# Mixture of experts: dense over all tokens, against rows sorted by expert through DRAM

## The chip, the cores and the metric

One core of a Trainium2 chip runs the whole program once. The metric is the device time of one execution in microseconds, the median of three runs. Engines are PE (matrix products), DVE (vector), ACT (scalar), POOL (general purpose) and SP, which here only issues DMAs.

## The reference, cut to what matters

Two transformer layers work on 32 x 141 = 4512 tokens of width 128. The change is in the last block, a mixture of 8 experts of hidden width 256 with the best 2 chosen for each token, and a shared expert that all tokens pass:

```python
xt = x.reshape(Bb * Ss, D)
shared = jax.nn.silu(xt @ sw1) * (xt @ sw3) @ sw2
scores = xt @ gate_w.T
_, idx = jax.lax.top_k(scores + biases, K)          # K = 2 of E = 8
topv, _ = jax.lax.top_k(scores, K)
p = jax.nn.sigmoid(topv)
p = p / jnp.sum(p, axis=-1, keepdims=True)
h = jax.nn.silu(jnp.einsum('td,edh->eth', xt, w1)) * jnp.einsum('td,edh->eth', xt, w3)
y = jnp.einsum('eth,ehd->etd', h, w2)
comb = jnp.einsum('tk,tke->te', p, onehot)
out = jnp.einsum('te,etd->td', comb, y) + shared     # + h outside
```

The reference itself computes every expert for every token and weights six of eight with zero.

## The kernel before, in words

The engines run programs of their own and meet by semaphores; the order on each engine is the order in which its lines are written. The residual stream `hT` and the normed input `xn` lie in SBUF with the feature on the partition and all 4512 tokens along the row. Until the last layer norm ("lnm") the kernel computes the tokens, the first attention, a merged feed-forward and the second attention; the change leaves those stages as they are, apart from a barrier point (`cleared`) at which semaphores of early stages are set to zero and used again, and from the layout of the expert weights `wparts`.

All fp32 products of the last block are made of three products in the type fp32r: a value is split into a high part (a cast) and a low part (value minus high part), and high x high, high x low and low x high are added up in PSUM (`three`, lines 876 to 879).

**Router.** In "lnm", chunk by chunk (12 chunks of 376 tokens), PE multiplies the gate weights by the chunk (L417), ACT copies the 8 x 376 scores (L425), PE turns them in four pieces (L413), and DVE gathers them (L431). POOL makes the low part of the input (L601). Then DVE computes the choice and the shares in one chain of dependent ops over 94 x 384 values (L1339 to L1395), PE turns the matrix of shares (L858), and ACT and DVE copy it.

**Expert stage.** For each chunk there are 18 units: 2 halves of the hidden width for each of the shared expert and the 8 experts. In one unit PE makes 3 gate-up products and 3 up products (L877 to L879); ACT applies silu (L1075); DVE multiplies by the share of the expert, which PE has broadcast to all partitions (L910, L1420), and by the up product (L1424); ACT casts the high part (L1068); POOL subtracts for the low part (L609); and PE makes 3 down products three units later, summed over all 18 units in one PSUM bank. Behind each chunk DVE adds the residual (L1407), PE turns the result in four pieces (L873), ACT copies it (L1063) and SP stores it (L401). The store's SBUF side is 94 partitions of 4 x 128 values, its DRAM side rows of 128 values:

```python
o = out.rearrange("b n d -> (b n) d").rearrange("(c s p) d -> c p s d", s=NSUB, p=SUB)   # SUB = 94, NSUB = 4
...
sp.dma_start(o[bass.ds(c, 1)].rearrange("a p s d -> (a p) s d"), m_o[0:SUB]).then_inc(S("stored"), 16)
```

Of the kernel before, what the change touches and what calls it, by code (L numbers as in the profile page):

```python
# [55 lines left out]
for _name, _n in (("ident", 128), ("centre", 128), ("average", 128), ("pos", NP_), ("jmask", 8),  # L56
                  ("hmask", H), ("vmask", 128), ("tmask", HT), ("dsel", NTAIL), ("rep", 72),
                  ("rank", E), ("select", E * 128)):
    CONST[_name] = (_at, _n)
    _at += _n  # L60
# [12 lines left out]
UN = 2 * (E + 1)  # L73
ORDER = [E] + list(range(E))
MEETINGS = ["ln1", "lnf"]
NORMS = ["ln1", "ln2", "lnf", "lna", "lnm"]
# [21 lines left out]

def run_steps(eng, units, lag, body, head):
# [12 lines left out]

def live(t, k, units):

    return not is_known(t) or 0 <= t - k < units


def early_fusion(nc, x, txt, tok, attn0, ffn, attn1, moe, const, out):
    with ExitStack() as ctx:
# [3 lines left out]
        sems = {}  # L123

# [92 lines left out]
        wparts = sb("wparts", [P, 2, 3 * (E + 1) * HID], F32R)  # L217
# [29 lines left out]
        xh = sb("xh", [P, T], F32R)  # L247
        xl = sb("xl", [P, T], F32R)
        m_ct = sb("m_ct", [P, T], F32R)
        selr = sb("selr", [P, E * P], F32R)  # L250
        m_bias = sb("m_bias", [P, E])
        router = ctx.enter_context(ExitStack())
        m_sc = sb("m_sc", [P, 2, CH], scope=router)
        m_s = sb("m_s", [P, NCH * NSUB, E], scope=router)
        m_t = [sb(f"m_t{i}", [P, NCH * NSUB, E], scope=router) for i in range(4)]
        m_1 = [sb(f"m_1{i}", [P, NCH * NSUB], scope=router) for i in range(5)]
        m_p = [sb(f"m_p{i}", [P, NCH * NSUB, E], scope=router) for i in range(3)]
        m_chi = sb("m_chi", [P, NCH * NSUB, E], F32R, scope=router)
        m_c40 = sb("m_c40", [P, NCH * NSUB, KC], scope=router)
        router.close()  # L260
        m_cb = sb("m_cb", [P, 2, CH])
        m_a = sb("m_a", [P, 3, CH])
        m_g = sb("m_g", [P, 3, CH])
        m_hf = sb("m_hf", [P, 3, CH])
        m_hh = sb("m_hh", [P, 3, CH], F32R)
        m_hl = sb("m_hl", [P, 3, CH], F32R)
        m_f = sb("m_f", [P, CH])
        m_o = sb("m_o", [P, NSUB, D])

        def expert(part, kind, e, k):  # L270

            at = (kind * (E + 1) + e) * HID + k * P
            return wparts[:, part, at:at + P]
# [51 lines left out]
        def _(sp):  # L325
            first = CONST["select"][0]
# [29 lines left out]
            sp.dma_start(cst[0:KC, first:], const[0:KC, first:]).then_inc(S("select_in"), 16)  # L356
# [29 lines left out]
            meet(sp, "lnf")  # L386

# [7 lines left out]
            sp.dma_start(m_bias[0:SUB, :], moe["biases"].unsqueeze(0).to_broadcast([SUB, E])).then_inc(S("bias_in"), 16)  # L395
            o = out.rearrange("b n d -> (b n) d").rearrange("(c s p) d -> c p s d", s=NSUB, p=SUB)

            sp.sem_inc(S("stored"), 16)
            with sp.Fori(0, NCH) as c:
                sp.wait_ge(S("out_copied"), c + 1)  # L400
                sp.dma_start(o[bass.ds(c, 1)].rearrange("a p s d -> (a p) s d"), m_o[0:SUB]).then_inc(S("stored"), 16)  # L401
            sp.wait_ge(S("stored"), 16 * (NCH + 1))

        def route_pe(pe, t, done):

            if 0 <= t - 1 < NCH:
                pe.wait_ge(S("r_sc"), t)
                if t >= 2:  # L410
                    pe.wait_ge(S("r_s"), t - 1)
                for s in range(NSUB):
                    mm = pe.transpose(bank[7][0:SUB, s * E:(s + 1) * E], m_sc[0:E, (t - 1) % 2, s * SUB:(s + 1) * SUB], ident[0:E, 0:E])  # L413
                mm.then_inc(S("r_tr"), 1)
            if 0 <= t < NCH:
                pe.wait_ge(S("ln_out"), done + t + 1)
                pe.matmul(bank[6][0:E, 0:CH], W("gate")[:, 0:E], chunk(xn, t), start=True, stop=True).then_inc(S("r_mm"), 1)  # L417

        def route_act(act, t):

            if 0 <= t < NCH:
                act.wait_ge(S("r_mm"), t + 1)
                if t >= 2:
                    act.wait_ge(S("r_tr"), t - 1)
                act.copy(m_sc[0:E, t % 2, :], bank[6][0:E, 0:CH]).then_inc(S("r_sc"), 1)  # L425

        def route_dve(dve, t):

            if 0 <= t < NCH:
                dve.wait_ge(S("r_tr"), t + 1)  # L430
                dve.tensor_copy(m_s[0:SUB, t * NSUB:(t + 1) * NSUB, :], bank[7][0:SUB, 0:NSUB * E].rearrange("p (s e) -> p s e", e=E)).then_inc(S("r_s"), 1)  # L431

        def ln_pe(pe, name):
# [32 lines left out]
            for t in range(NCH + 1):  # L468
                body(t, t % 4)
                if name == "lnm":  # L470
                    route_pe(pe, t - 3, done)
            if name == "lnm":
                for t in range(NCH - 2, NCH + 1):
                    route_pe(pe, t, done)

        def ln_act(act, name):
# [5 lines left out]
            for t in range(NCH + 2):  # L482
# [14 lines left out]
                if name == "lnm":  # L497
# [997 lines left out]
```

## Time and profile before

| | |
|---|---|
| median of 3 runs | 1076.8 us |
| all runs | 1075.12, 1076.8, 1141.8 us |
| span of the profiled execution | 1073.2 us |
| PE, DVE, ACT, POOL busy | 93%, 65%, 58%, 39% |
| DMA moved | 16.39 MB, mean 15 GB/s |

The profiled execution's own time beside its span is not recorded; the span runs from its first to its last instruction, and the median of the runs is 3.6 us longer. The page gives busy shares over the whole span; the stages differ, so the windows are to be read by stage: 613 to 645 us is the layer norm with the router's scores, 645 to 660 us the choice on DVE, 660 to 670 us the turning of the shares, and from there to 1066 us the expert stage.

### The profile page before, as it was taken

To read this page: it belongs to the slowest core of one execution; us is meant where nothing else is said; L and a number is where in the kernel's file an instruction comes from. 1 tells how busy PE (TensorE), PEld (TensorE's weight loads), DVE (VectorE), ACT (ScalarE), POOL (GpSimd) and SP (SyncE) were. 2 spreads that over 40 slices of the span, in tenths; PEclk is the share of its full clock that TensorE was granted. 3 is DMA by queue.
4 is the path that set the end of the run, shared out by engine and by line. 5 is a ranking of instruction groups with operands and counts; after the bars stand their busy time and mean duration, and the time that the engine had idled before them with its cause. 6 is when DMAs were issued, how large, how long until landed. Compare 5 with 4: busy or idle time off the path is not lost.

```text
span 1073.2 us, 20762 instructions
## 1 busy us (share of the span) xinstructions
PE 999.4 (93%) x5692; PEld 813.6 (76%) x5692; DVE 695.3 (65%) x1632; ACT 625.9 (58%) x1792; POOL 413.8 (39%) x469
## 2 busy tenths in 40 slices
PE   4789999989999689999999994999999999999996
PEld 3356666678898358888888733898988888988985
DVE  4835555489654958888888646656656566656663
ACT  5363333756655676666666472666666666566663
POOL 0100000068432443333333140555555555555553
PEclk9889999989999889999999995999999999999998
DMA  7000000013002200000000000000000000000000
GB/s 198 5 22 1 0 0 0 1 56 88 12 0 77 56 0 2 0 0 0 0 0 0 1 1 1 1 8 6 3 7 7 7 7 2 6 7 7 7 8 7
DMA packets 20010, 16.39 MB, mean 15 GB/s; under 512 B 3567, under 2 KB 17240, under 8 KB 19721
## 3 DMA queue, kind: packets, MB, share of 16 engines
q1 hardware_dynamic: 19977, 15.99, 5.2%
q8 instruction: 16, 0.26, 0.1%
q14 instruction: 17, 0.14, 0.0%
HBM read 13.68 MB, written 2.31 MB: 15 GB/s over the span
## 4 chain that ended last, share of the span: by engine, by line
PE 46%; issue 23%; POOL 20%; DVE 5%; ACT 4%; POOLq 1%; DMA 1%; SPq 0%; DVEq 0%; ACTq 0%
POOL m_hl L609 20%; PE ps3a L831 6%; PE ps L848 6%; PE ps3b L815 3%; PE ps3b L786 1%; PE ps3a L786 1%; PE ps L776 1%; PE ps3a L776 1%; DVE hT L524 1%; PE ps L698 1%; PE ps3b L720 1%; PE ps3a L727 1%; PE ps3a L729 1%; PE ps L821 1%; DVE arena L1142 1%
## 5 line engine op out<-in xcount | busy, mean ns | idle before, releaser
L609 POOL TENSOR_TENSOR m_hl<-m_hf,m_hh 128x376 fp32r<-128x376 f32 x216 | 216.9, 1004 | 201.7 <-ACT m_hh L1068 200.9
L1420 DVE TENSOR_TENSOR m_g<-m_a,m_cb 128x376 f32<-128x376 f32 x192 | 115.4, 601 | 111.1 <-ACT m_a L1075 110.5
L1043 ACT ACTIVATE arena<-ps3a,arena 128x141 f32<-128x141 f32 (+1 forms) x288 | 104.3, 391 | 43.2 <-DVE arena L1288 43.2
L1075 ACT ACTIVATE m_a<-ps3a 128x376 f32<-128x376 f32 x144 | 69.7, 484 | 90.0 <-PE ps3b L879 49.2
L586 POOL TENSOR_TENSOR arena<-arena,cst 128x1128 f32<-128x1128 f32 x32 | 66.3, 2073 | 134.4 <-ACT arena L1031 125.6
L1068 ACT CAST m_hh<-m_hf 128x376 fp32r<-128x376 f32 x216 | 107.9, 500 | 11.4 <-DVE m_hf L1424 11.4
L877 PE MATMUL ps3a<-xh,wparts 128*128 (+1 forms) x216 | 79.9, 370 | 0.0
L877 PE MATMUL ps3b<-m_hh,wparts 128*128 128x376 f32 x216 | 73.4, 340 | 1.3 <-POOL m_hl L609 1.2
L878 PE MATMUL ps3b<-m_hl,wparts 128*128 128x376 f32 x216 | 72.3, 335 | 0.0
L879 PE MATMUL ps3b<-m_hh,wparts 128*128 128x376 f32 x216 | 72.0, 333 | 0.0
L878 PE MATMUL ps3a<-xl,wparts 128*128 (+1 forms) x216 | 72.0, 333 | 0.0
L879 PE MATMUL ps3a<-xh,wparts 128*128 (+1 forms) x216 | 71.9, 333 | 0.0
L831 PE MATMUL ps3a<-arena 128*128 128x423 f32 (+1 forms) x192 | 68.3, 491 | 1.6 <-issue 1.6
L848 PE MATMUL ps<-arena 128*128 128x141 f32 x512 | 67.2, 283 | 1.9 <-DVE hT L1283 1.9
L848 PEld LDWEIGHTS ps<-arena 128*128 128x128 f32 x512 | 63.7, 190 | 2.3 <-ACT arena L1035 2.3
L1075 ACT ACTIVATE m_a<-ps 128x376 f32<-128x376 f32 x72 | 34.8, 484 | 49.8 <-PE ps L879 49.7
L561 POOL TENSOR_TENSOR mg_low<-tvc,mg_high 128x256 fp32r<-128x256 f32 x64 | 46.3, 743 | 43.6 <-DVE mg_high L1224 43.6
L1043 ACT ACTIVATION_READ_ACCUMULATOR arena<-ps3a,arena 128x1 f32 (+1 forms) x288 | 63.1, 219 | 0.0
L1288 DVE TENSOR_REDUCE arena<-ps3a 128x3 f32<-128x423 f32 x96 | 54.3, 593 | 7.9 <-PE ps3a L831 4.7
L554 POOL COPY arena<-xn 128x141 f32 (+1 forms) x32 | 9.7, 305 | 119.1 <-PE ps3b L721 100.8
L831 PEld LDWEIGHTS ps3a<-arena 128*128 128x128 f32 x192 | 34.9, 194 | 24.2 <-issue 24.2
L877 PE MATMUL ps<-xh,wparts 128*128 (+1 forms) x144 | 51.1, 355 | 0.1
(334 smaller groups left out, 2714.1 us busy)
## 6 DMA issues: line engine op xcount, KB each, us to landing
tvc<-in_L_ffn_tv_W_dram SPq DMA_DIRECT2D x32, 128.0 KB
out_dram<-m_o SPq DMA_DIRECT2D x12, 188.0 KB
arena<-in_x_dram SPq DMA_DIRECT2D x2, 1024.0 KB, 7.5
wraw_e<-in_L_ffn_w_dram SPq DMA_DIRECT2D x2, 1024.0 KB, 6.7
arena<-in_txt_dram SPq DMA_DIRECT2D x1, 1232.0 KB
wraw_e<-in_L_ffn_w_dram SPq DMA_DIRECT2D x2, 512.0 KB, 7.2
tvc<-in_L_ffn_W_dram SPq DMA_DIRECT2D x32, 16.0 KB
cst<-shape_constants SPq DMA_DIRECT2D x1, 394.5 KB, 3.3
```

Source lines behind the costliest of these rows:

```text
L586: pool.tensor_tensor(b_km[:, r], b_k[:, r, :].unsqueeze(1).to_broadcast([P, H, N]), C("hmask").unsqueeze(2).to_broadcast([P, H, N]), ALU.m ...
L609: pool.tensor_tensor(m_hl[:, s, :], m_hf[:, s, :], m_hh[:, s, :].bitcast(F32), ALU.subtract).then_inc(S("m_lo"), 1)
L831: mm = pe.matmul(ps3a[:, g, 0:n * N], b_q[:, q, 0:P], b_km[:, q, 3 * g:3 * g + n, :].rearrange("p h n -> p (h n)"), start=True, stop=True)
L848: pe.matmul(o, b_v[:, q, h, :], b_et[:, q, h, :], start=h == 0, stop=False)
L877: pe.matmul(dst, expert(0, kind, e, k), high, start=start, stop=False)
L878: pe.matmul(dst, expert(0, kind, e, k), low, start=False, stop=False)
L879: return pe.matmul(dst, expert(1, kind, e, k), high, start=False, stop=stop_)
L1043: ins = act.activation(b_e[0:rows, q, h, :], ps3a[0:rows, h // 3, (h % 3) * N:(h % 3) * N + N], ACT.Exp, bias=b_nm[0:rows, q, h:h + 1], ac ...
L1068: act.copy(m_hh[:, v % 3, :], m_hf[:, v % 3, :]).then_inc(S("m_hi"), 1)
L1075: act.activation(m_a[:, s, :], bank[2 * s][:, 0:CH], ACT.Silu).then_inc(S("m_silu"), 1)
L1288: dve.tensor_reduce(b_nm[:, q, 3 * g:3 * g + 3], ps3a[:, g, 0:3 * N].rearrange("p (h n) -> p h n", h=3), AX, ALU.max, negate=True).then_in ...
L1420: dve.tensor_tensor(m_g[:, s, :], src, m_cb[:, e % 2, :], ALU.mult).then_inc(S(used_up), 1)
```

## The change

Each token is now computed by the shared expert and by its two experts only.

- **Scores and rows.** In "lnm" PE multiplies three tiles of 128 tokens by the identity and the gate weights beside each other (136 columns), which gives each token's row and its 8 scores with the token on the partition. ACT copies them into `xr`, POOL copies the rows once more into `xr2`. The gate product, its copies and turns, and the split of the input by DVE and POOL in this stage go.
- **Positions.** DVE's choice works on 128 x 288 values. Then come a running count of the tokens of each expert (six shifted additions), two small products on PE for the counts over partitions, the number of tiles of 384 rows for each expert, each token's two positions `m_at` in a list sorted by expert, and a table `m_et` with the expert of each of the 31 tiles (31 is what the worst distribution needs). Each expert's last tile is filled up with rows of zeros.
- **DRAM.** `rows_by_expert` (31 x 384 rows of 130 values: the row, its share, its destination) is filled with zeros by two DMAs from SP after the second attention, and then POOL scatters all rows to their positions with 72 indirect DMAs of 128 rows.
- **Steps.** 12 shared steps (one chunk each) are followed by 31 routed steps (one tile each) in one pipeline. For a routed step SP loads the tile's rows, and copies the expert's up weights (128 x 1024) and down weights (128 x 512) from SBUF to SBUF, the expert read from the table into a register (`TENSOR_LOAD`). PE turns the rows in, makes the 18 products of a step, and turns the result out two steps later. DVE now makes all low parts, ACT all high parts. DVE scales the rows by the share and POOL scatters them by token into `rows_by_token` with three indirect DMAs a tile. The broadcasts of the shares go. The shared result is added to `hT` in SBUF.
- **End.** When all rows are scattered SP loads for each chunk both experts' results (24 loads of 94 x 512), POOL or DVE adds them, PE turns `hT`, DVE adds it, and SP stores the chunk (12 stores of 94 x 512).

What stands in a row on POOL, before, from the router on: the clearing of a table, the low parts of the input, and the loop of low parts of `m_hf`.

```order
L597 MEMSET m_c 128x1920
L601 TENSOR_TENSOR xl<-xn,xh 128x376 x12
L610 UNCONDITIONAL_BRANCH
L610 ISA
L609 TENSOR_TENSOR m_hl<-m_hf,m_hh 128x376
L608 REGISTER_ALU
L609 TENSOR_TENSOR m_hl<-m_hf,m_hh 128x376
L608 REGISTER_ALU
```

And now: the end of the second attention, clearing, the copies of rows, then DMAs with positions in SBUF. `xr,m_at` are a tile of rows and its positions, `yrow,homei` the results of a tile and their destinations.

```order
L709 COPY arena<-xn 128x104
L714 MEMSET m_c 128x256 x2
L717 COPY xr<-xr 128x3x128 x12
L724 DMA rows_by_expert<-xr,m_at 11904x130 x72
L731 DMA rows_by_token<-yrow,homei 9792x128 x93
L737 TENSOR_TENSOR ysum<-ysum 94x512 x6
L167 UNCONDITIONAL_BRANCH
```

The 216 subtractions over 376 columns went to DVE; in their place POOL has 72 + 93 indirect DMAs.

What stands on SP, before, from the second attention's end on: the bias and the loop of stores.

```order
L395 DMA m_bias<-in_L_ffn_biases_dram 94x8
L399 UNCONDITIONAL_BRANCH
L399 ISA
L401 ISA
L401 DMA out_dram<-m_o 94x4x128
L399 REGISTER_ALU
L399 COMPARE_AND_BRANCH
```

And now, a routed step inside the loop (rows, up weights, down weights of tile i):

```order
L484 DMA xrow<-rows_by_expert 128x390
L488 ISA
L488 TENSOR_LOAD m_et
L488 ISA x2
L119 ISA
L491 ISA
L491 DMA wb<-wparts 128x1024
L495 TENSOR_LOAD m_et
L495 ISA x2
L498 ISA
L498 DMA wb<-wparts 128x512
```

The row at L484 that begins the next step stands behind the down weights (L498), which wait for a down product of PE. At the program's end SP has, behind the last tile:

```order
L495 ISA x2
L498 ISA
L498 DMA wb<-wparts 128x512
L524 DMA ysum<-rows_by_token 94x512
L525 DMA ysum<-rows_by_token 94x512
L524 DMA ysum<-rows_by_token 94x512
L525 DMA ysum<-rows_by_token 94x512
...
L524 DMA ysum<-rows_by_token 94x512
L525 DMA ysum<-rows_by_token 94x512
L528 DMA out_dram<-ysum 94x512 x12
```

The stores, one behind each chunk before, now all come after the 24 loads.

The diff, cut to its core:

```diff
@@ sync engine
+            def load_rows(i, q):
+                g = NSH + i
+                at_least(sp, S("x_tp"), i - 1)
+                at_least(sp, S("homes"), i - 1)
+                sp.dma_start(xrow[:, q], rows[bass.ds(i, 1)].rearrange("a p s c -> (a p) s c")).then_inc(S(f"xrow_in{q}"), 16)
+            def load_w13(i, q):
...
+                e = sp.value_load(m_et[0:1, bass.ds(i, 1)], min_val=0, max_val=E - 1)
+                if not (is_known(i) and i < 2):
+                    at_least(sp, S("uu"), 2 * g - 2)
...
+            def load_w2(i, q):
...
+                e = sp.value_load(m_et[0:1, bass.ds(i, 1)], min_val=0, max_val=E - 1)
+                if not (is_known(i) and i < 2):
+                    at_least(sp, S("dn"), 2 * g - 2)
...
+            sp.wait_ge(S("scattered"), 16 * 2 * XT)
+            load_rows(0, 0)
+            load_rows(1, 1)
+            with sp.Fori(0, (RT - 3) // 2) as n:
+                for r in range(2):
+                    i = n * 2 + (2 + r)
+                    load_rows(i, r)
+                    load_w13(i, r)
+                    load_w2(i, r)
...
+            o = out.rearrange("b n d -> (b n) d").rearrange("(c p s) d -> c p (s d)", s=NSUB, p=SUB)
+            y1 = yt[0:T].rearrange("(c p s) d -> c p (s d)", s=NSUB, p=SUB)
+            y2 = yt[T:2 * T].rearrange("(c p s) d -> c p (s d)", s=NSUB, p=SUB)
+            sp.wait_ge(S("y_out0"), 16 * MS * ((RT + 1) // 2))
+            sp.wait_ge(S("y_out1"), 16 * MS * (RT // 2))
+            for c in range(NCH):
+                sp.dma_start(ysum[0:SUB, c, 0], y1[c]).then_inc(S(f"y_in{c}"), 16)
+                sp.dma_start(ysum[0:SUB, c, 1], y2[c]).then_inc(S(f"y_in{c}"), 16)
+            for c in range(NCH):
+                sp.wait_ge(S("o_done"), c + 1)
+                sp.dma_start(o[c], ysum[0:SUB, c, 1]).then_inc(S("stored"), 16)
@@ gpsimd
+            for i in range(XT):
+                n = P if i < XT - 1 else LASTX
+                for k, src in enumerate((xr, xr2)):
+                    pool.indirect_dma_start(xs[:, :], bass.IndirectOffsetOnAxis(ap=m_at[0:n, k, i:i + 1], axis=0),
+                                            src[0:n, i, 0:RW], None, oob_is_err=True).then_inc(S("scattered"), 16)
+            def send_rows(j, q):
+                pool.wait_ge(S("homei_set"), j + 1)
+                pool.wait_ge(S("yrow"), j + 1)
+                for s in range(MS):
+                    pool.indirect_dma_start(yt[:, :], bass.IndirectOffsetOnAxis(ap=homei[:, q, s:s + 1], axis=0),
+                                            yrow[:, q, s, :], None, oob_is_err=True).then_inc(S(f"y_out{q}"), 16)
@@ tensor
+            def moe_pe(g, r, now, prev, ahead, back):
+                if now == "routed":
+                    at_least(pe, S(f"w13_in{r}"), 8 * (g - NSH - r) + 16)
+                if now:
+                    up(g, r, 0, now == "shared")
+                if prev:
+                    down(g - 1, 1 - r, 0, prev == "shared")
+                if ahead:
+                    turn_in(g + 1 - NSH, 1 - r)
+                if now:
+                    up(g, r, 1, now == "shared")
+                if back:
+                    turn_out(g - 2 - NSH, r)
+                if prev:
+                    down(g - 1, 1 - r, 1, prev == "shared")
@@ scalar: silu, high part (k = 0), split of the next input, silu, high part (k = 1), copy of the down product
@@ vector: product, `homes` copy, low part (k = 0), low part of the next input, product, scaling of turned rows, low part (k = 1)
```

## Rows read from the trace of the kernel before

**Rows 1.** The page: span, busy times, and granted PE clock in 40 slices.
```profile
span 1073.2 us, 20762 instructions
...
PE 999.4 (93%) x5692; PEld 813.6 (76%) x5692; DVE 695.3 (65%) x1632; ACT 625.9 (58%) x1792; POOL 413.8 (39%) x469
...
PEclk9889999989999889999999995999999999999998
```

**Rows 2.** Windows: router, expert stage; busy us (instructions), PEclk, DMA share, GB/s.
```profile
645.00:660.00 15.00, 0.34 (x4) 0.25 (x4) 13.65 (x38) 0.79 (x3) 0.00 (x0) 0.55 0.00 1
...
670.00:1066.00 396.00, 393.65 (x2083) 350.16 (x2082) 238.75 (x420) 240.95 (x540) 216.91 (x216) 1.00 0.02 6
```

**Rows 3.** Waits, 700 to 1073 us: who waited for whom, us, times, longest.
```profile
POOL m_hl L609 <- ACT m_hh L1068: 162.1, 196, 1.7
DVE m_g L1420 <- ACT m_a L1075: 100.6, 151, 1.0
```

**Rows 4.** Timeline, PE in the expert stage: start, us, instruction.
```profile
1043.11 0.33 PE L877 MATMUL ps3b<-m_hh,wparts 128*128 128x376 f32 x1
1043.28 0.33 PE L878 MATMUL ps3b<-m_hl,wparts 128*128 128x376 f32 x1
```

**Rows 5.** Chain that ended last, 600 to 640 us: layer norm steps and attention products.
```profile
600.56 1.93 PE ps L848 x16
...
602.89 1.06 PE ps3b L815 x8
...
633.68 0.73 PE ps3b L417 x2
634.41 0.83 PE ps3a L461 x2
635.24 0.63 PE ps3b L467 x2
```

**Rows 6.** Timeline, DVE at the router: start, us, instruction, idle before.
```profile
645.38 0.19 DVE L431 COPY m_s<-ps3b 94x32 f32<-94x32 f32 x1 [1.44 <-PE ps3b L413]
...
650.08 0.55 DVE L1341 TENSOR_TENSOR m_t<-m_t,cst 94x384 f32<-94x384 f32 x1
...
655.46 0.18 DVE L1373 TENSOR_SCALAR m<-m 94x48 f32<-94x48 f32 x1
```

**Rows 7.** Windows, DMA share and GB/s: first loads, and the last store.
```profile
12.00:13.00 1.00, 0.56 (x3) 0.59 (x4) 0.30 (x1) 0.98 (x4) 0.00 (x0) 1.00 0.98 379
...
1067.00:1072.40 5.40, 0.00 (x0) 0.00 (x0) 0.00 (x0) 0.00 (x0) 0.00 (x0) 0.50 0.13 36
```

**Rows 8.** The page, costliest groups: busy, mean ns, idle before.
```profile
L609 POOL TENSOR_TENSOR m_hl<-m_hf,m_hh 128x376 fp32r<-128x376 f32 x216 | 216.9, 1004 | 201.7 <-ACT m_hh L1068 200.9
L1420 DVE TENSOR_TENSOR m_g<-m_a,m_cb 128x376 f32<-128x376 f32 x192 | 115.4, 601 | 111.1 <-ACT m_a L1075 110.5
...
L586 POOL TENSOR_TENSOR arena<-arena,cst 128x1128 f32<-128x1128 f32 x32 | 66.3, 2073 | 134.4 <-ACT arena L1031 125.6
L1068 ACT CAST m_hh<-m_hf 128x376 fp32r<-128x376 f32 x216 | 107.9, 500 | 11.4 <-DVE m_hf L1424 11.4
```

**Rows 9.** SP: a large and the last issue (timeline), and its wait for that store.
```profile
344.32 0.44 SPq L392 DMA_DIRECT2D wraw_e<-in_L_ffn_w_dram  x1
...
1066.33 0.24 SPq L401 DMA_DIRECT2D out_dram<-m_o  x1
...
SPq L119 <- DMA out_dram<-m_o: 6.1, 1, 6.1
```

**Rows 10.** DMA issues: KB each, median us from issue to landing.
```profile
cst<-shape_constants SPq DMA_DIRECT2D x1, 394.5 KB, 3.3
...
vec<-in_L_attn_bk_dram SPq DMA_DIRECT2D x1, 0.5 KB, 2.3
```

**Rows 11.** Timelines of DVE and POOL, 353 us: two ops side by side.
```profile
353.35 4.97 DVE L524 SCALAR_TENSOR_TENSOR hT<-xn,vec,hT 128x376 f32<-128x376 f32 x1
...
352.88 5.04 POOL L578 TENSOR_TENSOR wparts<-wraw_e,wparts 128x2304 fp32r<-128x2304 f32 x1 [9.94 <-DVE wparts L510]
```

More of the change, by code:

```diff
@@ L110, in run_steps, with moe_steps, at @@
         body(t, t % 2)
+def moe_steps(eng, body):
+    last = NSH + RT - 1
+    def at(g):
+        now = "shared" if g < NSH else "routed" if g <= last else None
+        prev = None if g == 0 or g - 1 > last else "shared" if g - 1 < NSH else "routed"
+        return now, prev, NSH <= g + 1 <= last, NSH <= g - 2 <= last
+    for g in range(2):
+        body(g, g % 2, *at(g))
+    with eng.Fori(0, (NSH - 4) // 2) as n:
+        for r in range(2):
+            body(n * 2 + (2 + r), r, "shared", "shared", False, False)
+    for g in range(NSH - 2, NSH + 4):
+        body(g, g % 2, *at(g))
+    loops = (RT - 6) // 2
+    with eng.Fori(0, loops) as n:
+        for r in range(2):
+            body(n * 2 + (NSH + 4 + r), r, "routed", "routed", True, True)
+    for g in range(NSH + 4 + 2 * loops, last + 3):
+        body(g, g % 2, *at(g))
 def live(t, k, units):
@@ L402, in _ @@
[L402 to L417, printed above, removed]
@@ L615, in _ @@
+            for j in range(RT):
+                send_rows(j, j % 2)
+            for c in range(0, NCH, 2):
+                pool.wait_ge(S(f"y_in{c}"), 32)
+                pool.tensor_tensor(ysum[0:SUB, c, 1], ysum[0:SUB, c, 0], ysum[0:SUB, c, 1], ALU.add).then_inc(S("y_pair"), 1)
         @block.tensor
@@ new lines, in moe_act @@
+            def moe_act(g, r, now, prev, ahead, back):
+                n = CH if now == "shared" else M
+                for k in range(2):
+                    u, s = 2 * g + k, 2 * r + k
+                    if now:
+                        at_least(act, S("ug"), u + 1)
+                        at_least(act, S("prod"), u - 3)
+                        act.activation(h_s[:, s, 0:n], bank[GB_[k]][:, 0:n], ACT.Silu).then_inc(S("silu"), 1)
+                        at_least(act, S("prod"), u + 1)
+                        at_least(act, S("dn"), u - 3)
+                        act.copy(h_hi[:, s, 0:n], h_f[:, s, 0:n]).then_inc(S("h_hi"), 1)
+                    if k == 0 and (ahead or (now == "shared" and is_known(g) and g + 1 < NSH) or (now == "shared" and not is_known(g))):
+                        split_x(g + 1, 1 - r, "routed" if ahead else "shared")
+                if prev == "routed":
+                    at_least(act, S("dn"), 2 * g)
+                    at_least(act, S("y_tp"), g - 1 - NSH - 1)
+                    act.copy(yT[:, 1 - r, :], bank[YB][:, 0:M]).then_inc(S("y_taken"), 1)
@@ new lines, in _, with rest_x @@
+            dve.wait_ge(S("ends"), 1)
+            chain(dve.tensor_tensor(m_j[0:1, :, :], C("turn", 1).unsqueeze(2).to_broadcast([1, RT, E - 1]),
+                                    m_e[3][0:1, 0:E - 1].unsqueeze(1).to_broadcast([1, RT, E - 1]), ALU.is_ge))
+            chain(dve.tensor_reduce(m_f[0:1, :], m_j[0:1, :, :], AX, ALU.add))
+            dve.tensor_copy(m_et[0:1, :], m_f[0:1, :]).then_inc(S("table"), 1)
+            def rest_x(g, q, kind):
+                src, n = (chunk(xn, g), CH) if kind == "shared" else (bank[XB][:, 0:M], M)
+                at_least(dve, S("x_hi"), g + 1)
+                dve.tensor_tensor(x_lo[:, q, 0:n], src, x_hi[:, q, 0:n].bitcast(F32), ALU.subtract).then_inc(S("x_lo"), 1)
```

538 lines of the change are left out of this document (300 added, 238 removed).

## The prediction, made before the changed kernel ran

> **What bounds the kernel now.** I read the page's head first: the kernel spans 1073.2 us, PE is busy 93% of it and POOL, the least used, 39% [rows 1]. The windows by stage come next. The router, 645 to 660 us, is a stretch in which DVE alone works (13.65 of 15 us, PE 0.34) and the clock falls to its lower level. The expert stage, 670 to 1066 us, has PE busy 393.7 of 396 us at the full clock, DVE and ACT about 60%, POOL 55% [rows 2]. The waits inside it are those of engines that have slack: POOL waits 162.1 us for ACT's high part, DVE 100.6 us for silu, and PE shows next to none [rows 3]. So the stage is bound by PE: 12 chunks x 18 units x 9 matmuls = 1944 matmuls with a start every 0.17 us (0.172 over a unit) [rows 4] is 334 us, the rest being the 96 share broadcasts and the gaps around them. A change that takes 60% of the matmuls away therefore hits the right engine, and the question is what becomes late in its place.
>
> **The change, part by part.** Times count from the start of the span; the sum is made against 1073.2 us. The median of the three runs is 3.6 us above that, which I add at the end.
>
> (a) Layer norm before the router. PE sets its step: 0.73 (gate product) + 0.83 + 0.63 and four small turns, 2.47 us a chunk [rows 5]. The gate product and the turns go, and three products with 136 columns come. One of 141 columns in 8 pairs took 1.93 us, so 0.24 each, 0.7 in all. Saved: 0.3 us x 12 = 3.5. The last scores, now read at 645.4 [rows 6], are there at 642. POOL loses 12 low parts and gets 12 copies that nobody waits for in this stretch.
>
> (b) Router on DVE. It is a chain: 0.55 us for an op over 384 columns (start to start 0.59), 0.18 for a small one [rows 6]. The width falls from 384 to 288 columns, which I price at 0.46 start to start. The two choices, 12 ops, fall from 7.0 to 5.6 us; the tree of maxima and the shares keep about 5; the running count adds 8 wide ops (3.7), positions and table 6 wide and some 14 narrow ones of 0.2 (5.6), and two products on PE. Sum about 20, so the positions are there at 660.5 and the table, for which ACT waits, at 662. The split and transposed share matrix, 660 to 668 us, falls away [rows 2], so the first expert matmul comes at 663.5 instead of 668. Clearing 6.2 MB of DRAM from 614.7 us on lasts 16 us at the best rate seen (379 GB/s [rows 7]) and would be hidden even at half of it.
>
> (c) Shared expert, 12 steps. PE needs 18 x 0.172 = 3.1 us. DVE has six ops of 0.55 to 0.60, 3.5 us, and twice waits for ACT's high part (0.50 [rows 8]) of a product it has just made, partly filled: 4.3 us a step. It ends at 663.5 + 52 = 715.
>
> (d) 72 scatters on POOL, of 128 rows each. No row shows POOL making a DMA's descriptors. Below, SP's own issue of one takes 0.24 us; SP's large ones 0.44 [rows 9]. POOL's ops over 128 partitions take 1.00 us (376 columns) and 2.07 us (1128) [rows 8]. I take 1.3, next to the 1.00 row, because POOL builds the rows in software; the range keeps 0.24 and 2.07. They end at 660.5 + 93.6 = 754, landed 2.3 us later (the shortest landing shown [rows 10]). The shared expert, done at 715, covers 52 of these 96 us; the routed tiles can't start without all of them. A row load (3.3) and what PE has left to do in the last shared step (2.4) follow: the first routed tile starts at 762.
>
> (e) 31 routed steps. Compute alone: DVE adds the scaling of the rows and two small copies to (c), ACT the copy of the down product, about 4.8 us; PE 3.15 + six transposes (8 took 1.06 [rows 5], so 0.8). But SP issues rows, up weights and down weights in this order and waits before the down weights of one tile until the down product two steps back has ended. The rows of the next tile stand behind that wait. From that end: issue 0.44, the rows' landing 2.8 (between 2.3 for 0.5 KB and 3.3 for 394 KB [rows 10]), 0.7 for the 256 KB ahead of them in the queue (379 GB/s). At 3.95 us PE can turn the rows in (0.4), do the second up half (1.03), turn out (0.4), and the down product (0.52): 2.35. That closes the loop at 6.3 us; with the bounds 2.3 + 0 and 3.3 + 0.7 for landing it is 5.1 to 6.8. POOL's three scatters, 3 x 1.3 = 3.9, fit. 31 x 6.3 = 195: the last tile ends at 957. What drains behind it (high part, down product, copy, turn, scaling, three scatters, landing) is 9 us: 966.
>
> (f) The end. Before, the last chunk is stored while nothing else remains: issued at 1066.3, waited for 6.1 us [rows 9]. During it the DMA share is 0.13 and the rate 36 GB/s, where loads of 128 partitions reach 0.98 and 379 GB/s [rows 7]. So a transfer from 94 partitions runs on 2 of 16 engines. Eleven of the twelve stores lay beside the chunks. Now 24 loads of the same 94 partitions (188 KB = 192.5 kB each), and then the 12 stores, come after the last scatter with no cover left. With 2 KB runs I price an engine at the best rate, 379/16 = 23.7 GB/s: 192.5 kB / 47.4 GB/s = 4.06 us; x 36 = 146, and 4 us for the first issue and last landing: 150. (At the 5.4 us of the store with its 512 B runs it would be 194.) The adds and turns on POOL, DVE and PE lie beside it.
>
> The Trainium skill, "DMA: Bandwidth & Descriptors", section on why a DMA increments its semaphore by 16, says that a copy is split over the largest number of engines up to 16 that divides the slowest dimension of both sides. That gives 2 for 94 rows, for the loads as for the store; the trace shows it for the store alone (0.13), so the rule speaks against this change exactly where the rows leave the loads open.
>
> Sum: 966 + 150 = 1116, + 3.6 = 1119 us. Up to the point where only the end is left the change gains 100 us (966 against 1066); the end takes back 143 (150 against 7).
>
> **Rivals.**
> 1. *Loads on all engines* (other side). If only the store's DRAM side, whose rows are pieces of 512 B, kept it to two engines, 36 transfers at 379 GB/s take 18 us and the end 25 instead of 150: 994 us, faster by 8%. For: the loads and new stores have contiguous DRAM. Against: the SBUF side is still 94 partitions. It decides for "faster" as soon as the end costs less than 85 us.
> 2. *POOL cheap and the step at compute speed.* Scatter 0.45 us, so the shared expert ends last (715), step 4.8: 716 + 149 + 8 + 150 + 3.6 = 1027. For: SP's 0.44. Against: the order of SP's waits. With only the scatter cheap and the step at 6.3 it is 716 + 195 + 8 + 150 + 3.6 = 1073, no change.
> 3. *POOL kept waiting by DVE.* DVE's op on L524 took 4.97 us instead of 0.61 while POOL's 5.04 us subtraction ran [rows 11]: one engine shuts the other out. If each scatter waits for one DVE op (0.55): 72 x 0.55 = 40 more, 1159; in the routed steps 5.55 < 6.3 stays hidden. At 2.07 per scatter 72 x 0.77 = 55 and 2.5 of drain: 1177.
> 4. *Clock.* With PE at two thirds of a step busy and waiting in between, the clock may stay at its lower level, as at 645 to 660 us [rows 2]. PE's 2.35 us become 4.3, the step 8.25: 31 x 1.95 = 60 more, 1180. Against: most slices with gaps kept 8 or 9 tenths [rows 1].
>
> The Trainium skill, "SBUF — State Buffer", its warning that DVE blocks a DMA issued from GpSimd, gives 620 ns alone and 3100 ns beside a fp32 copy. Worked through as an estimate on that page's figure, scatters of 3.1 us would take 223 us the routed step 9.3, and the kernel would end near 1350; the only such copies here are of a few columns, so it weighs on rival 3's chance and not on its price.
>
> **How the numbers follow.** Forecast case 0.42 (own range 1080 to 1160, from the step's 5.1 to 6.8 and scatters of 1.0 to 1.7); rival 3 0.22; rival 4 0.07; cheap scatters alone 0.11; rival 2 proper 0.08; rival 1 0.10. Predicted 1119. The range 1060 to 1185 leaves out rivals 1 and 2 proper, and the far ends of (f) and of rival 3. A change is told from none at 2%, 1055 to 1098 us: faster = 0.10 + 0.08 = 0.18; same = 0.11 and a little of the forecast case = 0.12; slower 0.70.
>
> **What would show it.** Right: loads of ysum at a DMA share near 0.13 for about 100 us at the end, then stores; PE idle between 715 and 760; a routed step of 6.3 us with PE waiting for the row DMA before its first turn. Wrong: a share near 1 in the last loads; scatters on POOL far from 1.3 us; routed steps in which DVE has no gap (4.8) or in which POOL is without one (over 2.1 us a scatter). Most would turn on (f): a short end makes the whole change a gain.

## The result, and the profile after

The changed kernel took 1133.2 us (median of 5 runs, 1128.5 to 1198.2) beside 1076.8 us of the kernel before on the same chip: a ratio of 1.052, 95% interval 1.048 to 1.056. The forecast was 1119 us, slower. Run again later (e12 and e8 below) it gave 1.033 (1.021 to 1.046), with a lowest run of 1113.9 us, and 1.076 (1.066 to 1.086). Some executions of every kernel here, the one before included, show a lower mean granted clock and take several per cent longer; the ratios compare executions without that, the medians hold all of them.

The profiled execution of the first try spans 1196.2 us: in it the granted clock stood at 0.50 from 100 to 200 us, ahead of everything the change touches, and from the first scatter on it agrees with the others. I therefore read the rows from another execution of the same kernel, run e12, span 1120.3 us. From the first scatter to the end of the span it is 457.0 us in e12, 454.5 in the first profile and 453.1 in e5.

The heads of the two pages, first try and then e12 (PEclk in 40 slices), answer to [rows 1]:

```profile
span 1196.2 us, 17719 instructions
...
PEclk9775555559999988999999996975988888965555
```

```profile
span 1120.3 us, 17719 instructions
...
PE 798.1 (71%) x4568; PEld 641.1 (57%) x4568; DVE 611.8 (55%) x1543; ACT 498.5 (44%) x1491; POOL 357.8 (32%) x427
...
PEclk9899999999998899999999959858888888855555
```

PE's busy time falls by 201 us against [rows 1], and the kernel is slower: no engine is busy for even three quarters of the span.

The windows of e12 by stage (shared steps, scatters alone, routed steps, loads of the end, stores of the end) answer to [rows 2, 7]. Columns: busy us of PE, PE's weight loads, DVE, ACT, POOL; PEclk; DMA share; GB/s.

```profile
663.00:715.00 52.00, 40.51 (x201) 35.69 (x201) 34.64 (x69) 28.03 (x59) 39.77 (x40) 0.93 0.23 81
715.00:756.00 41.00, 0.00 (x0) 0.00 (x0) 0.00 (x0) 0.00 (x0) 30.66 (x33) 0.54 0.16 51
760.00:960.00 200.00, 145.63 (x718) 129.19 (x717) 103.02 (x237) 86.17 (x180) 77.86 (x81) 0.88 0.49 169
980.00:1063.00 83.00, 4.38 (x16) 2.61 (x16) 10.30 (x15) 0.00 (x0) 6.28 (x5) 0.51 0.13 49
1063.00:1119.00 56.00, 0.00 (x0) 0.00 (x0) 2.06 (x3) 0.00 (x0) 1.26 (x1) 0.50 0.13 51
```

Three stretches in which PE is short of work took the place of one in which it was full: 41 us with scatters alone, routed steps with PE busy 73%, and 142 us of transfers at a DMA share of 0.13, the share that the one store before had [rows 7].

The waits of e12 from 660 us on, first the engines', then SP's queue, answer to [rows 3, 9]. Before, POOL and DVE waited for ACT, and PE for next to nothing (1.2 us for POOL); now the rows' DMA stands ahead of PE, and a PE product ahead of SP's down weights:

```profile
POOL rows_by_token L731 <- DVE yrow L1566: 111.4, 28, 22.9
...
PE ps3b L1022 <- DMA xrow<-rows_by_expert: 97.7, 29, 44.6
```

```profile
SPq L498 <- PE ps3a L987: 95.6, 29, 4.5
SPq L484 <- DMA rows_by_expert<-xr,m_at: 87.9, 1, 87.9
```

Of PE's 97.7 us, 44.6 are the one gap behind the scatters; 53 us in 28 parts are the routed steps'.

### The profile page after: what moved, and what is told of

Same layout as the page of the kernel before. It is cut to its first block, busy times and chain, and to the rows that moved or that the text cites. A ratio compares the mean times of both kernels' runs of the same rounds, so it can differ in the third digit from the quotient of the medians.

```text
span 1196.2 us, 17719 instructions
## 1 busy us (share of the span) xinstructions
PE 873.8 (73%) x4568; PEld 680.1 (57%) x4568; DVE 611.9 (51%) x1543; ACT 497.5 (42%) x1491; POOL 358.3 (30%) x427
## 4 chain that ended last, share of the span: by engine, by line
PE 54%; SPq 8%; DMA 8%; issue 8%; DVE 7%; POOL 7%; ACT 4%; POOLq 0%; DVEq 0%; ACTq 0%
DMA xrow<-rows_by_expert 6%; POOL rows_by_expert L724 6%; PE ps L974 5%; PE ps3a L957 5%; SPq L524 3%; SPq L525 3%; PE ps3b L941 3%; PE ps L823 2%; PE ps3b L845 2%; PE ps3a L852 2%; PE ps3a L854 2%; PE ps3a L985 2%; PE ps3a L987 2%; PE ps3a L986 2%; PE ps3b L1022 1%
## 5 line engine op out<-in xcount | busy, mean ns | idle before, releaser
L731 POOL DMA_INDIRECT rows_by_token<-yrow,homei x93 | 89.2, 959 | 129.1 <-DVE yrow L1566 108.3
L1022 PE MATMUL ps3b<-cst,xrow 128*128 128x128 f32 x93 | 17.7, 301 | 98.5 <-DMA xrow<-rows_by_expert 98.5
L724 POOL DMA_INDIRECT rows_by_expert<-xr,m_at x72 | 71.1, 988 | 40.8 <-issue 21.6
L1205 ACT CAST h_hi<-h_f 128x384 fp32r<-128x384 f32 (+1 forms) x86 | 43.9, 511 | 74.0 <-DVE h_f L1557 67.8
L1022 PEld LDWEIGHTS ps3b<-cst,xrow 128*128 128x128 f32 x93 | 10.1, 145 | 107.8 <-DMA xrow<-rows_by_expert 107.7
L1571 DVE TENSOR_TENSOR h_lo<-h_f,h_hi 128x384 fp32r<-128x384 f32 (+1 forms) x86 | 47.8, 556 | 16.8 <-ACT h_hi L1205 15.9
L1193 ACT CAST x_hi<-ps3b 128x384 fp32r<-128x384 f32 x31 | 14.8, 479 | 96.3 <-PE ps3b L1022 96.3
L1117 ACT COPY arena<-ps3b 128x256 f32<-128x256 f32 x32 | 11.9, 372 | 102.1 <-PE ps3b L846 102.1
L1316 DVE SCALAR_TENSOR_TENSOR hT<-ps3a,vec,hT 128x141 f32 (+1 forms) x32 | 11.7, 365 | 73.9 <-PE ps3a L854 73.9
L1420 DVE TENSOR_TENSOR arena<-arena 128x1024 f32<-128x1024 f32 x32 | 39.1, 1220 | 0.0
L1401 DVE COPY arena<-ps3b 128x512 f32<-128x512 f32 x32 | 22.2, 693 | 27.5 <-PE ps3b L944 27.5
```

Of the source, the lines that this page charges most:

```text
L724: pool.indirect_dma_start(xs[:, :], bass.IndirectOffsetOnAxis(ap=m_at[0:n, k, i:i + 1], axis=0), src[0:n, i, 0:RW], None, oob_is_err=True) ...
L731: pool.indirect_dma_start(yt[:, :], bass.IndirectOffsetOnAxis(ap=homei[:, q, s:s + 1], axis=0), yrow[:, q, s, :], None, oob_is_err=True).t ...
L1022: mm = pe.transpose(bank[XB][:, s * P:(s + 1) * P], xrow[:, q, s, 0:D], ident)
L1205: act.copy(h_hi[:, s, 0:n], h_f[:, s, 0:n]).then_inc(S("h_hi"), 1)
L1420: dve.tensor_tensor(b_e[:, r, 0:8, 0:P], b_e[:, r, 0:8, 0:P], b_r[:, r, 0:8].unsqueeze(2).to_broadcast([P, H, P]), ALU.mult)
L1571: dve.tensor_tensor(h_lo[:, s, 0:n], h_f[:, s, 0:n], h_hi[:, s, 0:n].bitcast(F32), ALU.subtract).then_inc(S("h_lo"), 1)
```

## The experiments

Twelve runs, each beside the kernel before on its chip. There were four chips: e1 to e4 and e12 ran on one, e5 to e7, e8 and e9, e10 and e11 on one each. Spans are compared from the first scatter on, since the stages ahead of it are the same in all variants of the changed kernel and vary by their clock.

### e1 and e7: the end over 96 partitions

```diff
+OUTS = [(384 * c, 4) for c in range(11)] + [(4224, 3)]
+OP = 96
...
-                sp.dma_start(ysum[0:SUB, c, 0], y1[c]).then_inc(S(f"y_in{c}"), 16)
+                sp.dma_start(ysum[0:OP, c, 0, 0:OUTS[c][1] * D], token_rows(yt, 0, c)).then_inc(S(f"y_in{c}"), 16)
```

(and the same for the second load, the adds, the turns and the stores: the same tokens in 11 pieces of 96 x 4 and one of 96 x 3).

> The end's loads and stores run over 96 partitions (11 pieces of 96 x 4 tokens and one of 96 x 3) instead of 94; nothing else changes. Theory A (94 partitions let a transfer run on 2 of 16 engines only, and the end of 36 such transfers, 142 us, stands uncovered): the DMA share in the end rises from 0.13 to well over 0.5, the end takes about 22 us (issue of 24 loads at 0.35 us, a chain of adds of some 12 us on DVE, then 12 stores), the kernel about 1010 us, faster than before. Rival B (the rate of the end is set by DRAM rows that POOL has just written, or by SP): the share stays near 0.13 and the time near 1133 us. Rival C (the engine count goes with the number of partitions in proportion): 96 instead of 94 changes 2%, 1130 us.

e1: median 1033.5 us (1011.2 to 1050.1), profile 1018.6. From the last send (987.8 us) to the end it is 30.8 us, where the changed kernel has 144.2. A window of the end's loads (the share adds up the times of the packets, so it can read over 1) and one of SP's issues in e1:

```profile
992.00:1002.00 10.00, 4.18 (x15) 2.42 (x15) 4.39 (x7) 0.00 (x0) 3.78 (x3) 0.53 1.01 269
```

```profile
992.81 0.41 SPq L528 DMA_DIRECT2D ysum<-rows_by_token  x1
```

The changed kernel, e12:

```profile
979.00 0.39 SPq L524 DMA_DIRECT2D ysum<-rows_by_token  x1
979.43 4.25 SPq L525 DMA_DIRECT2D ysum<-rows_by_token  x1
983.72 3.79 SPq L524 DMA_DIRECT2D ysum<-rows_by_token  x1
```

The first three issues pass at 0.3 to 0.4 us, then each takes as long as a transfer, 3.9 us: SP stands at its queue, which I read as full. With 96 partitions no issue took more than 0.43 us. The same bytes over two partitions more take 113 us less.

> The kernel with 96 partitions in the end, once more, since its four runs lay between 1011 and 1050 us. Theory A: the end costs 22 to 30 us instead of 142, so a ratio of about 0.94 to the kernel before (1011 against 1076). If the spread is the clock in the early stages, the lowest runs agree within 1% and the stages from the router on are alike in all profiles.

e7: median 1018.7 us (1001.6 to 1093.4, 7 runs), ratio 0.935 (0.928 to 0.942): the changed kernel with this one edit beats the kernel before.

### e6: the end over 92 partitions

```diff
+OUTS = [(368 * c, 4, 92) for c in range(12)] + [(4416, 1, 96)]
```

> The end in 12 pieces of 92 x 4 tokens and one of 96 x 1. Theory A (a transfer runs on the largest number of engines up to 16 that divides its partitions: 2 for 94, 4 for 92, 16 for 96): the share in the end is near 0.25, each transfer of 188 kB takes 188.4 / 94.8 = 2.0 us instead of 3.9, the 36 of them 72 us, the end about 78 us, the kernel 142 - 78 = 64 us below the changed one, near 1068 us. Rival (any count that is no multiple of 16 or 32 gets two engines): share 0.13, 1133 us. Rival (the gain of 96 came from 32-row alignment or from nearly full use of the partitions): 92 is like 94, no change.

Median 1058.6 us (1047.1 to 1064.6), ratio 0.976 (0.971 to 0.981); from the last send (987.9) to the end of the span (1062.3) 74.4 us. The loads' window:

```profile
992.00:1031.00 39.00, 4.83 (x17) 2.76 (x17) 8.93 (x13) 0.00 (x0) 6.28 (x5) 0.51 0.26 98
```

Shares 0.13, 0.26 and 1.01 and ends of 144, 74 and 31 us for 94, 92 and 96 partitions: fewer partitions (92) are twice as fast as 94, so not their number but what divides it decides. Three counts do not tell whether every divisor up to 16 counts or only the powers of two, for 2, 4 and 16 are both. The loads have contiguous DRAM in all three, which is where rival 1 falls.

### e2: SP issues the next rows ahead of the down weights

```diff
             load_rows(1, 1)
+            load_rows(2, 0)
             with sp.Fori(0, (RT - 3) // 2) as n:
                 for r in range(2):
                     i = n * 2 + (2 + r)
-                    load_rows(i, r)
                     load_w13(i, r)
+                    load_rows(i + 1, 1 - r)
                     load_w2(i, r)
```

> SP issues the row load of the next tile before it waits for the down weights of this one; the end is as in the changed kernel. Theory A (the loop of 6.3 us a routed step runs over SP's wait for the down weights and the row load queued behind it): a step falls to about 5.1 us, between the compute of 4.8 and the up weights' chain of 5.6, 31 steps give 35 us, time about 1098 us; PE no longer waits for xrow. Rival B (the step is bound by DVE and ACT, the wait for rows only shows it): no change, 1133 us. Rival C (the DMA engines are shared by the weights' copies): PE waits for the up weights instead, gain under 10 us.

Median 1081.0 us (1064.2 to 1151.9, 10 runs), ratio 0.991 (0.984 to 0.998). A routed step takes (916.9 - 774.4)/30 = 4.75 us instead of 6.5 to 6.6. SP's queue in it, and the window of the routed steps:

```profile
853.02 0.49 SPq L491 DMA_DIRECT2D wb<-wparts  x1
853.76 0.38 SPq L484 DMA_DIRECT2D xrow<-rows_by_expert  x1
857.02 0.50 SPq L498 DMA_DIRECT2D wb<-wparts  x1
```

```profile
774.00:917.00 143.00, 123.89 (x717) 111.49 (x716) 95.53 (x237) 78.60 (x179) 76.67 (x80) 0.99 0.69 231
```

The rows are asked for 1.7 or 3.3 us ahead of the down weights, PE waits for them once only (the gap behind the scatters), and the clock in these steps rises from 0.88 to 0.99 with it. Another wait takes a part of the old one's place, as rival C had it for its mechanism though not for its size: PE waits 18.8 us in 16 parts for the up weights. So these steps alternate too, with the clock at 1.00: by the starts of PE's turns (L1022), 4.2 us without that wait and some 5.4 with it.

### e3 and e10: both edits

> Both edits, 96 partitions in the end and rows first. If the two terms are separate places in time their gains add: about 1010 - 35 = 975 us. If the faster steps only run into POOL's scatters of results (3 x 1.26 = 3.8 us a step) nothing is lost either, since the step stays above it.

e3: median 961.9 us (954.5 to 967.6), ratio 0.893 (0.885 to 0.901). From the first scatter to the end 288.1 us: against the changed kernel's 454 to 457 that is 113 from the end and some 53 from 30 steps, so the two add up. Windows of shared steps, scatters alone, routed steps and end:

```profile
663.00:715.00 52.00, 39.71 (x201) 35.05 (x201) 35.47 (x72) 27.94 (x59) 39.08 (x39) 0.94 0.23 78
715.00:756.00 41.00, 0.00 (x0) 0.00 (x0) 0.00 (x0) 0.04 (x1) 31.21 (x33) 0.52 0.16 53
760.00:905.00 145.00, 124.87 (x720) 112.53 (x721) 96.53 (x238) 79.06 (x180) 76.87 (x80) 0.98 0.68 230
905.00:953.00 48.00, 16.52 (x88) 13.15 (x86) 17.68 (x34) 3.97 (x9) 20.55 (x20) 0.67 0.59 181
```

Only the 41 us of scatters alone are left as they were.

> Both edits together, a third time. The second time (spans from 1013 us) stood 60 us over the first (952 us): its trace shows each signal from PE to ACT and DVE coming some 8 us after the one before while POOL scatters in the shared steps, and the shared steps lasting to 793 us instead of 711. Theory: that belongs to the one chip: here the shared steps take 4.2 us each again and the runs stand at 952 to 970. Rival: it belongs to the kernel and can come anywhere: a part of the runs here, over the same chip, stand at 1015 or above while others stand under 970.

e10, on another chip: median 961.7 us (954.2 to 969.2, 6 runs), ratio 0.891 (0.885 to 0.898).

### e4: half of the scatters

The 36 scatters of each token's second row are left out, and the end reads the first results twice, so the second expert's share of the sum is not computed:

```diff
-                for k, src in enumerate((xr, xr2)):
+                for k, src in enumerate((xr,)):
```

> Leaves out the 36 scatters of each token's second row (those rows stay zeros in the list, and the end reads the first results twice); all steps and transfers after it are the same. Theory A (72 scatters at 1.26 us start to start end 43 us after the shared expert, with PE idle): the scatters end at about the time of the shared steps, the routed steps start some 40 us sooner, time about 1093 us. Rival B (something else, such as the clearing of DRAM or the weights' table, holds the first tile): 1133 us. Rival C (DVE's ops over SBUF lengthen the scatters that run beside the shared steps): the 36 that are left take over 1.5 us each and the gain is under 25 us.

Median 1094.5 us (1070.0 to 1160.9). The scatters in its trace (ns min/median/max, first and last start):

```profile
L724 POOL DMA_INDIRECT rows_by_expert<-xr,m_at x36: 864/959/1284, 679.3 to 725.5; - x36
```

The first routed tile is split 51.3 us after the first scatter instead of 96.7 in e12, 45 us sooner, and from the first scatter to the end it is 406.6 us, 47 to 50 less than the 453.1 to 457.0 of the changed kernel. Each scatter taken away gives back its full 1.26 us: that chain, and not the shared expert, sets when the routed steps begin.

### e11: scatters behind the shared steps

```diff
+            pool.wait_ge(S("uu"), 2 * NSH - 1)
             for i in range(XT):
```

> Both edits, and POOL's first scatter waits until PE has made the first up products of the last shared step, so that shared steps and scatters don't run side by side. Where PE's signals come in time: the scatters start 48 us after the router and all 92 us lie behind the shared steps, so the kernel takes 47 to 50 us longer than both edits alone (1000 to 1017). Theory for a chip on which the signals come late beside scatters: the shared steps take 4.2 us again, the 60 us lost there come back, and this kernel is within 15 us of both edits alone. Rival: the signals are late there for a reason other than the scatters, and this kernel is 48 us slower than both edits alone there too.

Four runs of 1002.5 to 1048.2 us; the lowest stands 48.3 us above the lowest of both edits alone on this chip (954.2). The traces, whose early stages ran at different clocks, give the same from the last cast of the positions to the end: 1045.2 - 708.1 = 337.1 us against 953.4 - 664.6 = 288.8. That is as expected where PE's signals come in time. So the shared steps do cover some 50 us of scatters. What it was to tell on a chip with late signals stays open, for this chip had none.

### e5, e8, e9 and e12: the same kernels again

> The changed kernel once more, unedited, for a profile in which the early stages run at full clock (in the first one PE stood at 0.50 between 100 and 200 us). Both theories expect the same of it: about 1130 us, the stages from the router on as in the first profile (scatters 1.26 us start to start, routed step 6.3 to 6.5 us, end about 142 us), and the excess of the first profile all ahead of the router.

e5 took 1183.9 us, with the clock at 0.50 from 100 to 200 us as in the first profile, and 453.1 us from the first scatter to the end.

> The changed kernel unedited, for the 14 us between its median (1133.2) and the forecast (1119). Theory: the part from the first scatter to the end lasts 453 to 455 us whatever the run, and the difference lies in the stages ahead of the router, where the granted clock falls to about 0.56 in some runs from 75 us on and not in others (first scatter at 664 without it, at 675 to 680 with it): so the fastest of some six runs comes at 1116 to 1121 and others stand 11 to 14 us above it. Rival: the stages behind the router cost 14 us more than the profiled execution shows, and no run comes under 1126.

> Both edits together once more, on the same chip. Theory: from the first scatter to the end 287 to 289 us; runs at 952 to 958 where the clock stays up ahead of the router, and 964 to 970 where it doesn't; median 12% below the kernel before, whatever the share of the two. Rival: the first time was luck of one chip, and the median here is above 985.

Both were misses. e8: median 1163.6 us (1155.1 to 1204.0); e9: 1042.0 us (1015.1 to 1092.1), ratio 0.944 (0.935 to 0.952), on one chip where the kernel before ran as elsewhere (from 1077.1). The time is lost beside the scatters, in the shared steps, and for e9 in the routed ones too (5.7 us each). Timeline of e9 (on this kernel L989 and L991 are products, L1207 is silu, L1562 the product by the up half, L1210 the high part):

```profile
728.11 0.52 PE L991 MATMUL ps3a<-h_hi,wparts 128*128 128x376 f32 x1
732.89 0.48 ACT L1207 ACTIVATE h_s<-ps 128x376 f32<-128x376 f32 x1 [16.40 <-remote]
740.60 0.55 DVE L1562 TENSOR_TENSOR h_f<-ps,h_s 128x376 f32<-128x376 f32 x1 [16.22 <-remote]
741.18 0.51 ACT L1210 CAST h_hi<-h_f 128x376 fp32r<-128x376 f32 x1 [7.81 <-issue]
...
742.94 0.68 PE L989 MATMUL ps<-x_hi,wparts 128*128 128x376 f32 x1 [14.32 <-issue]
```

PE is done at 728.6, but silu begins at 732.9 and DVE, whose partner (silu) ended at 733.4, at 740.6. DVE to ACT takes 0.03 us as ever. What is late in the trace is what PE signals: ops that wait for PE start at 715.4, 723.8, 732.9 and 740.6, some 8 us apart. In none of the profiles from the other three chips does the trace name such a wait. Why one chip does this is not shown, and that the scatters bring it on is not either: the two only stand side by side.

> The changed kernel unedited once more, for the 14 us between its median (1133.2) and the forecast (1119), since the chip of the last try delayed PE's signals. Theory: first scatter to end 453 to 455 us, so that a run whose granted clock stays up ahead of the router (first scatter at 664, as in both edits together) takes 1117 to 1121, and the next ones stand 11 to 14 us above it. Rival: the changed kernel's runs have their floor at 1128 and none of seven comes under 1126; then the floor is 10 us higher than both edits' early part and my 664 don't hold for it.

e12: median 1135.9 us (1113.9 to 1161.7, 6 runs; the lowest three 1113.9, 1117.8, 1122.3), ratio 1.033 (1.021 to 1.046). The first scatter comes at 663.3 with PEclk 1.00 from 75 to 200 us; in e1, e2 and e6 it came at 677 with PEclk 0.55 or 0.56 from 75 to 100. The changed kernel has no floor at 1128. The other three took 1149.5 to 1161.7 us, well over the 11 to 14 us above the lower ones that the theory gave; they have no trace.

## Why the prediction was right, step by step

The span of e12 is 1120.3 us where the sum gave 1116, and with 2.0 us around it 1122.3 where the forecast was 1119.

**(a) Layer norm and (b) router.** DVE's timeline in e12, to set beside [rows 6]:

```profile
643.70 0.64 DVE L1476 TENSOR_TENSOR m_p<-xr 128x144 f32<-128x144 f32 x1 [2.45 <-ACT xr L553]
...
646.89 0.45 DVE L1464 TENSOR_REDUCE m<-m_t 128x36 f32<-128x288 f32 x1
647.38 0.46 DVE L1465 TENSOR_TENSOR m_t<-m_t,m 128x288 f32<-128x288 f32 x1
...
653.27 2.92 DVE L1500 TENSOR_TENSOR m_c<-m_c 128x288 f32<-128x288 f32 x6
...
662.19 0.18 DVE L1533 CAST m_at<-m 128x36 int32<-128x36 f32 x1
...
663.09 0.17 DVE L1538 CAST m_et<-m_f 1x31 int32<-1x31 f32 x1
```

The scores are read at 643.7, not 642: 1.7 us sooner than before, not 3.5. That is the difference of two misses. The stages ahead of the layer norm, which the forecast took as unchanged, end 3.9 us later. The new layout of `wparts` makes DVE's cast of the expert weights write nine runs of 256 columns in place of one of 2304, which is all that differs in it, and each of the three casts takes 2.55 us instead of 1.35. The first of them, the last product of the second attention, and the new product of the scores, before and then in e12:

```profile
351.44 1.35 DVE L510 CAST wparts<-wraw_e 128x2304 fp32r<-128x2304 f32 x1
...
610.92 2.17 PE ps L848 x16
```

```profile
351.61 2.55 DVE L630 CAST wparts<-wraw_e 128x2304 fp32r<-128x2304 f32 x1
...
614.77 2.17 PE ps L974 x16
...
623.98 0.69 PE ps3b L548 x6
```

Before the first cast DVE is 0.2 us behind, after the third 3.7. From that last product to the scores it is 643.7 - 614.8 = 28.9 us against 645.4 - 610.9 = 34.5 before, 5.5 saved where (a) had 3.5: a chunk takes 1.96 us (0.69, 0.63 and 0.63) in place of 2.47, 0.5 less and not 0.3, for the first product behind the gate's took 0.83 and takes 0.63 now. The wide op is 0.45 and 0.49 start to start (priced 0.46). Positions are there at 662.4 after 18.7 us of chain (660.5 and 18.5 forecast), the table at 663.3 (662). What these two steps miss lies ahead of the choice, not in it.

**(c) Shared steps.** (710.3 - 663.3)/11 = 4.27 us by the casts at their heads; 4.3 forecast. PE stands still from 715 us, as forecast.

**(d) Scatters.** POOL's timeline in e12:

```profile
663.35 1.16 POOL L724 DMA_INDIRECT rows_by_expert<-xr,m_at  x1 [19.16 <-DVE m_at L1533]
664.81 0.95 POOL L724 DMA_INDIRECT rows_by_expert<-xr,m_at  x1 [0.30 <-issue]
666.07 0.96 POOL L724 DMA_INDIRECT rows_by_expert<-xr,m_at  x1 [0.30 <-issue]
```

0.96 us and 0.30 between two: 1.26, and over all 72 (754.6 - 663.35)/71 = 1.29. That 1.3 met it is luck: it was taken from a subtraction on POOL [rows 8], and no row ahead of the run showed an indirect DMA; the range kept 0.24 and 2.07. They land 2.3 us later, and the first tile is turned at 759.1 (762 forecast). Rivals 2 (0.45 us) and 3 (+0.55) fall: in the first profile the 38 scatters beside shared steps took 1.02 us in the mean, the 34 behind them 0.95. The Trainium skill's warning ("SBUF — State Buffer", DVE blocks a DMA issued from GpSimd) gives 3100 ns for a DMA beside a copy on DVE. The DVE ops beside these scatters are products, sums and subtractions, and with them the trace shows 7%, not a factor; no wide copy ran beside them.

**(e) Routed steps.** The mechanism was right and its size is 0.3 short: (958.4 - 760.0)/30 = 6.61 us against 6.3. Two turns of the loop in e12:

```profile
851.95 0.49 SPq L498 DMA_DIRECT2D wb<-wparts  x1
852.70 0.38 SPq L484 DMA_DIRECT2D xrow<-rows_by_expert  x1
...
855.13 0.55 PE L1022 MATMUL ps3b<-cst,xrow 128*128 128x128 f32 x3 [1.71 <-DMA xrow<-rows_by_expert]
...
857.74 0.49 SPq L498 DMA_DIRECT2D wb<-wparts  x1
858.83 0.34 SPq L484 DMA_DIRECT2D xrow<-rows_by_expert  x1
...
861.26 0.73 PE L1022 MATMUL ps3b<-cst,xrow 128*128 128x128 f32 x3 [1.90 <-DMA xrow<-rows_by_expert]
...
865.45 0.49 SPq L498 DMA_DIRECT2D wb<-wparts  x1
```

0.75 from the weights' issue to the rows', 2.43 to the turn on PE, 2.61 to the next issue: 5.8 us; the forecast had 3.95 + 2.35 = 6.3, its way to the turn 0.8 too long and PE's part 0.3 too short. The second turn takes 1.09 + 2.43 + 4.19 = 7.7 us. From the seventh step on they alternate so: by the issues at L498, twelve turns of 7.65 to 7.86 us stand between ones of 5.8 to 6.0. Windows of PE's part in a long turn (from 847.77) and in the short one behind it:

```profile
846.00:848.00 2.00, 0.23 (x1) 0.23 (x2) 0.20 (x3) 0.51 (x1) 1.39 (x3) 0.96 0.68 211
848.00:850.00 2.00, 2.00 (x8) 2.00 (x8) 1.08 (x3) 0.84 (x2) 0.75 (x1) 0.50 0.72 254
850.00:852.00 2.00, 2.00 (x11) 1.90 (x10) 1.19 (x4) 0.73 (x3) 0.00 (x0) 0.69 0.00 0
...
856.00:858.00 2.00, 2.00 (x14) 1.79 (x13) 1.55 (x4) 1.18 (x3) 0.28 (x1) 1.00 0.58 205
```

After its wait for the rows PE works at 0.50, the lower level of 1.2 GHz, in every second step, 8 matmuls in 2 us instead of 14. PE's part takes 4.19 us there and 2.61 at the higher level, 1.6 more; the other 0.3 of a long turn is SP's issue of the rows, 1.09 us behind the weights' in place of 0.75, for a reason that is not shown. Twelve times 1.6 is 19 us, more than the step's whole miss of 31 x 0.3 = 10: without the lower level the step would have been near 6.0 us, below the forecast, so here too two misses cancel in part. That is rival 4, at a third of its price: it had the lower level throughout (60 us). The alternation alone would not show the clock, since e2's steps alternate at 1.00; PE's slower rate does. Compute alone was put at 4.8 us; e2's 4.75 is a mean that holds waits for the up weights, and its steps without such a wait take 4.2. From the end of the 31 steps (759.1 + 31 x 6.61 = 964) it is 12 us to the last scatter's start (976.1) and 2 more to the end's first load at 978.3: a drain of 14, with 9 forecast. That chain counted the three scatters of one tile; the last twelve, of four tiles, stand back to back on POOL from 962.2 us on.

**(f) The end.** Loads 3.92 us apart (4.06 forecast), 978.3 to 1120.3 = 142 us (150). Rival 1 falls with the share of 0.13. The rule of the Trainium skill ("DMA: Bandwidth & Descriptors", why a DMA increments its semaphore by 16: the largest number up to 16 that divides the slowest dimension of both sides) gives 2, 4 and 16 engines for 94, 92 and 96; the measured shares 0.13 and 0.26 and the three ends agree.

So two misses cancel in part: the end begins at 978.3 instead of 966, 12 us late (the steps 10 more, the drain 5 more, the first tile 3 sooner), and lasts 8 us less. The mechanism was right in each term that the sum named, but that the sum comes within 4 us of e12's time is in part luck: (d)'s price, and misses of opposite sign in (a), within (e), and between (e) and (f). The 14 us by which the first try's median stands over the forecast belong to no term of the sum: where a trace shows such a delay (e1, e2, e6), it lies ahead of the router, in the granted clock of 75 to 200 us. The 1130 us executions of the first try have no trace, so for them this is inferred. e8's median stands 45 us over the forecast, on the one chip with late signals, which no row ahead of the runs could show.

Where did the saving of 60% of the matmuls go? PE's busy time fell 201 us and the span grew 47, so PE stands idle 248 us longer. 41 us of it are the scatters alone, about 53 SP's order with its clock dips, 113 the split of the last transfers; most of the rest is the 31 us that the end takes even on all engines and the 14 of the drain. The 53 and the 113 are no price of sorting, as e3 shows.

## What to carry to other kernels

Before rows are moved through DRAM with no work beside the transfer, look at the partition count: by their shares 94 ran on 2 DMA engines, 92 on 4, 96 on all, 144, 74 and 31 us for the same data. On a queue that issues in order, put the load that the next step needs ahead of the one that must wait for a buffer; here this gave 1.8 us a step, and part of it as clock. When most of an engine's work goes, price the serial chains that were hidden beside it (here 72 indirect DMAs of 1.26 us), for they set the new time. And when a buffer's layout changes for a new reader, price its writer again: here three casts in an early stage lost 3.6 us.

## What the runs showed of the hardware

- On SP (e12) three loads were issued in 0.3 to 0.4 us each, and every one behind them took as long as a transfer: 3.9 us, and 1.9 us where transfers are faster (e6); at 0.43 us each (e1) none waited.
- DVE's cast of 128 x 2304 values takes 1.35 us into one run of columns and 2.55 us into nine runs of 256 (L510 before, L630 in e12).
- In the routed steps of e12, where PE waits some 2 us a step for its rows, the granted clock stood at its lower level after that wait in every second step (PEclk 0.50 from 848 to 850 us); with the rows asked for earlier (e2) the stage's was 0.99.
- The early stages, alike in the changed kernel's variants, ran at PEclk 1.00, 0.96 or 0.50 to 0.58 from 100 to 200 us, with the first scatter at 663 to 667, 677 to 679 and 709 to 742 us.
- On one chip of four, PE's signals reached ACT and DVE some 8 us apart while POOL issued scatters; the same two kernels lost 35 to 39 (e8) and 60 us (e9) there. The kernel before, which has no indirect DMA, took 1077.1 us there at its lowest and 1073.2 to 1074.1 on the other three.
